# Attention on one Trainium2 core: products of probabilities and values for two key tiles in one burst

## The reference, cut to what matters

```
x = x + attention0(layernorm(x), ctx, mask)        # stage xa0: cross attention, masked
x = x + block(layernorm(x))                        # stage sa0: self attention, then 8 experts (me0)
x = x + attention1(layernorm(x), ctx)              # stage xa1: cross attention
x = x + experts(x)                                 # me1

def attention(Q, K, V, mask, W_Q, W_K, W_V, W_O):
    q, k, v = split_heads(Q @ W_Q.T), split_heads(K @ W_K.T), split_heads(V @ W_V.T)
    scores = einsum('bhqd,bhkd->bhqk', q, k) / sqrt(DK)
    weights = softmax(where(mask == 0, -inf, scores))
    return merge_heads(einsum('bhqk,bhkd->bhqd', weights, v)) @ W_O.T
```

## Time and profile before

| what | value |
| --- | --- |
| median of 3 runs | 1273.53 us (1271.52 to 1274.54) |
| the profiled execution, its own time | 1274.43 us |
| its span | 1272.7 us |
| TensorE matmul busy | 1131.4 us, 89% of the span |
| VectorE busy | 838.6 us, 66% |
| ScalarE busy | 660.4 us, 52% |
| L985, 1536 records | 204.9 us busy, mean 605 ns |
| L958, 720 records, and L971, 768 | 280.9 and 294.3 us busy |

### The profile page before, as it was taken

The page is one execution under the profiler, slowest core; times in us unless marked ns, Lnnn a source line. Parts: engine busy times, 40 slices in busy tenths (PEclk is TensorE's granted clock), DMA queues, the critical chain, the costliest instruction groups (busy, mean ns, idle before and its releaser), DMA issues. The chain is left out here.

```text
span 1272.7 us, 17810 instructions
## 1 busy us (share of the span) xinstructions
PE 1131.4 (89%) x5693; PEld 544.0 (43%) x5722; DVE 838.6 (66%) x2112; ACT 660.4 (52%) x1341; POOL 210.9 (17%) x272
## 2 busy tenths in 40 slices
PE   7889999999997999999967999996989999998390
PEld 4423343434453223343364666664523333335370
DVE  5878777777478888888762222223888888876722
ACT  3346666666533677677722333332537767674250
POOL 4310000000143000000202222211520010102154
PEclk9989999999999899999967999998989999999795
DMA  8953321221048433543291140103873323211064
GB/s 265 309 169 93 79 57 28 81 52 26 2 154 291 103 91 90 132 97 93 72 375 33 31 161 28 27 13 102 263 241 91 90 59 89 60 37 57 25 171 144
DMA packets 100706, 139.40 MB, mean 110 GB/s; under 512 B 8452, under 2 KB 82632, under 8 KB 99208
## 3 DMA queue, kind: packets, MB, share of 16 engines
q1 hardware_dynamic: 96536, 128.03, 33.6%
q0 software_dynamic: 4080, 10.23, 2.9%
HBM read 86.30 MB, written 52.17 MB: 109 GB/s over the span
## 5 line engine op out<-in xcount | busy, mean ns | idle before, releaser
L885 ACT ACTIVATE r<-ps 128x512 f32<-128x512 f32 x768 | 427.4, 600 | 211.9 <-PE ps L971 122.1
L377 DVE TENSOR_REDUCE m<-ps 128x1 f32<-128x512 f32 x512 | 320.9, 682 | 45.2 <-PE ps L958 44.9
L971 PE MATMUL ps<-r 99*128 99x512 bf16 x768 | 294.3, 388 | 5.6 <-ACT r L885 5.6
L958 PE MATMUL ps<-r 96*128 96x512 bf16 x720 | 280.9, 393 | 20.5 <-DVE m L377 7.0
L373 DVE CUSTOM_DVE_ANT_0 r<-ps,r 128x512 bf16<-128x512 f32 x256 | 170.2, 690 | 60.2 <-PE ps L958 59.6
L985 PE MATMUL ps<-r 128*32 128x512 f32 x1536 | 204.9, 605 | 4.9 <-ACT r L885 3.3
L971 PEld LDWEIGHTS ps<-r 99*128 99x128 bf16 x768 | 74.4, 98 | 211.7 <-ACT r L885 157.3
L958 PEld LDWEIGHTS ps<-r 96*128 96x128 bf16 x720 | 71.3, 99 | 105.9 <-DVE m L377 24.3
L861 POOL COPY r<-r 128x256 f32<-128x256 f32 x48 | 19.0, 399 | 542.1 <-PE ps L985 542.1
L1660 DVE COPY r<-ps 128x512 f32<-128x512 f32 x46 | 31.8, 691 | 91.9 <-PE ps L1707 91.9
L1707 PE MATMUL ps<-r 128*128 x184 | 87.8, 621 | 2.7 <-issue 0.4
(11 more groups left out here) (151 smaller groups left out, 1220.5 us busy)
## 6 DMA issues: line engine op xcount, KB each, us to landing
r<-q_parts SPq DMA_DIRECT2D x48, 384.0 KB, 5.2
r<-k_parts SPq DMA_DIRECT2D x48, 384.0 KB, 6.0
k_parts<-r SPq DMA_DIRECT2D x24, 384.0 KB, 3.3
q_parts<-r SPq DMA_DIRECT2D x24, 384.0 KB, 3.1
r<-in_w SPq DMA_DIRECT2D x16, 512.0 KB, 4.9
r<-in_w SPq DMA_DIRECT2D x8, 1024.0 KB, 14.4
k_parts<-r SPq DMA_DIRECT2D x24, 256.0 KB, 3.3
q_parts<-r SPq DMA_DIRECT2D x24, 256.0 KB, 3.1
```

Source lines behind the costliest of these rows:

```text
L377: ins = dve.tensor_reduce(out, mem.ps[:, bank, :], AX.X, ALU.max)
L885: act.activation(mem.probs[:, u // HG, u % HG, :], ps[:, ST + (UNITS * g + u) % DEEP, :], ACT.Exp, scale=SCALE).then_inc(a.p_exp.sem, 1)
L958: pe.matmul(ps[:, led_bank(n), :], mem.qst[g][0:ROWS, h, t * P:(t + 1) * P], mem.kst[g][0:ROWS, h, :], start=True, stop=True).then_inc(a.s ...
L971: ins = pe.matmul(out, mem.kst[g][0:KROWS, h, kt * P:(kt + 1) * P], mem.qst[g][0:KROWS, h, :], start=True, stop=not a.masked)
```

## The change

`products` now makes two key tiles (`TOGETHER` = 2), eight matmuls in a row. It stands behind unit 9 for key tiles 0 and 1, and behind unit 1 of the next group for key tiles 2 and 3; the calls behind units 5 and 13 are gone. It waits for the exponentials of both key tiles before its first matmul. The semaphore `pv` still counts each key tile. At the end of a stage the last call makes two key tiles as well.

```
--- before.py
+++ after.py
@@ -754,6 +754,7 @@
 HALF_TURN = (3, 13)
 LAST_TURN, LAST_OUT = (5, 2), (3, 4)
 LATE = 2
+TOGETHER = 2
 
 M_STEP, TURN_STEP = 8, 12
 OUT_TURNS = (3, 5)
@@ -976,15 +977,16 @@
                             start=False, stop=True)
         ins.then_inc(a.st_ps.sem, 1)
 
-    def products(G, g, kt):
-        pe.wait_ge(a.p_exp.sem, a.p_exp.at(G, HG * (kt + 1)))
-        if kt == 0:
+    def products(G, g, first):
+        pe.wait_ge(a.p_exp.sem, a.p_exp.at(G, HG * (first + TOGETHER)))
+        if first == 0:
             pe.wait_ge(a.vg_ready.sem, a.vg_ready.at(G, 1))
             pe.wait_ge(a.ot_sb.sem, a.ot_sb.at(G))
-        for h in range(HG):
-            ins = pe.matmul(ps[h * VW:(h + 1) * VW, OB, :], mem.vg[g % 2][:, kt, h, :], mem.probs[:, kt, h, :],
-                            start=(kt == 0), stop=(kt == T - 1))
-        ins.then_inc(a.pv.sem, 1)
+        for kt in range(first, first + TOGETHER):
+            for h in range(HG):
+                ins = pe.matmul(ps[h * VW:(h + 1) * VW, OB, :], mem.vg[g % 2][:, kt, h, :], mem.probs[:, kt, h, :],
+                                start=(kt == 0), stop=(kt == T - 1))
+            ins.then_inc(a.pv.sem, 1)
 
     def maxima(G):
         pe.wait_ge(a.cut.sem, a.cut.at(G, CUTS))
@@ -1056,11 +1058,11 @@
                     used = before(b, UNITS * g + u)
                     scores(s, v, UNITS * g + u, (used[0], used[1] + LEAD))
 
-                at = u - HG - LATE + 1
-                if at < 0 and u == LATE - 1 and not (first and g == 0):
-                    products(G - 1, (g - 1) % NG, T - 1)
-                if at >= 0 and at % HG == 0:
-                    products(G, g, at // HG)
+                at = u + 1 - LATE
+                if at == 0 and not (first and g == 0):
+                    products(G - 1, (g - 1) % NG, T - TOGETHER)
+                if at > 0 and at % (TOGETHER * HG) == 0:
+                    products(G, g, at // HG - TOGETHER)
                 if g == 1 and not first and u in OUT_TURNS:
                     turn_out(b - 1, OUT_TURNS.index(u))
                 if u == M_STEP and not (last and g == NG - 1):
@@ -1100,7 +1102,7 @@
         body(b, False, False)
     body(B - 1, False, True)
     G = B * NG - 1
-    products(G, NG - 1, T - 1)
+    products(G, NG - 1, T - TOGETHER)
     turn(G)
     meanwhile()
     for c in range(1, C):
```

## The result

The changed kernel takes 1310.3 us (median of 4, 1304.99 to 1313.14) against 1274.03 for the kernel before on the same chip: a ratio of 1.028, interval 1.025 to 1.032, so 36 us slower. Forecast were 1306, 32 us slower.

A forecast was written before the change was run, and what follows sets the result against it. TensorE bounds the kernel, but merged bursts starve it through VectorE's slower maxima: 32.6 us in the unmasked stages, −2 in the first, +1.5 at stage ends, sum 32, so 1306 us; range 1288 to 1320.

The forecast's parts named there:

- What binds whom: Unmasked stages: TensorE sets the time; its bursts let VectorE (0.60 us per maximum against 0.44 per unit) catch up.
- The double burst: Two key tiles in one burst: lasts 1.90 us, saving 0.19 us per pair of bursts.
- Run B: Unmasked units 10 to 15, 0 and 1: eighth L958 waits for VectorE; 6.88 us instead of 6.12, 0.76 slower.
- Plain group: Unmasked group without other work, runs of 7.09 and 6.88 us: grows from 12.2 to 14.0 us.
- the walk: Step-by-step timing of eight-unit unmasked runs from trace spacings: units 2 to 9 lose 1.00 us, units 10 to 1 0.76.
- Over a batch boundary: First unit of a batch reuses the bank of the unit just before: 0.15 us more, three times per unmasked stage, 0.5.
- Groups with output tiles: Groups 2 and 3, units 2 to 9: 0.90 us slower in the second stage, 0 in the last.
- First stage: Masked stage: 28 double bursts save 5.3 us, against 2.4 for banks between batches and about 1 for mask copies; net −2.
- rival 2: Unmasked stages: waits of about 1 us per run drop TensorE's clock to 1.2 GHz in places; 1335 us; chance 0.04.
- Rival 1: All stages: TensorE stays the bound, every double burst among scores saves 0.19 us, nothing waits; 1258 us; chance 0.08.
- Rival 3: Inside a double burst the second quad doesn't follow directly: 2.18 us instead of 1.90, 24 more; 1330 us; chance 0.04.
- Rival 4: Waits and savings cancel: waits a quarter of those forecast, time within 0.2%, 1271 to 1276 us; chance 0.04.

The follow-up runs named there:

- e3: The changed kernel with maxima over half of the columns in the two unmasked stages; 1259.63 us, ratio 0.989 to the kernel before.
- e5: The changed kernel with double bursts behind units 13 and 5 and stacks loaded one group earlier; 1270.78 us, ratio 0.998 to the kernel before.
- e1: The kernel before with double bursts in the masked first stage alone, other two attention stages unchanged; 1265.17 us, ratio 0.992.

## Why the prediction was right, point by point

- **What binds whom: right.** TensorE set the time before, and only because single bursts let VectorE catch up. e3 (shorter maxima) and e5 (other places) both take the loss away with the double bursts in place. TensorE's busy share in the last stage fell to 91% and VectorE's to 79%, as forecast.
- **The double burst: right, a little long.** 1.86 instead of 1.90. The drain at a change of tiling that the Trainium skill describes ("TensorEngine Tiling (Array Packing)", Key Properties) would be saved once per pair. The trace agrees as far as it goes: groups of the masked stage with the output's turns went from 16.66 to 16.14, 0.26 per pair where I had 0.19; it shows the spacing of the records, not a drain by itself.
- **Run B: right.** 6.79 against 6.88. **Plain group: right in itself**, 13.85 against 7.09 + 6.88 = 13.97, but the kernel before had 12.69 and 12.84 there and not the walk's 12.21, so the loss is 1.0 to 1.2 and not 1.76. It waited for stacks, as I had seen, but I took only 0.2 per group off for that. Over a batch boundary the last stage lost 1.53 where my terms give 1.91; that remainder I haven't traced. Groups with the output's turns lost 0.84 (forecast 0.88).
- **Groups with output tiles.** Last stage 0.65 more (forecast 0.76), second stage 1.52 more (forecast 0.90 + 0.76 = 1.66).
- **First stage: sign right, size wrong.** Forecast −2, measured −6.4, and −7.5 in e1. The two terms against the saving hold: the copies of the mask cost 0.9 in the third group (15.74 before, 16.15 after, two L959 behind L373 late by 0.46 and 0.41; I had about 1), and a group over a batch boundary lost 0.15 where my terms, the bank less the saving, give 0.4. Too small was the saving, 0.24 to 0.26 per pair instead of 0.19, 7 us instead of 5.3. Left out were a wait of 0.8 for stacks (L958 at 97.53) that the changed kernel hasn't, and the burst that leaves the way to group 0: this way is 1.5 shorter, of which the burst is 1.31 − 0.22 = 1.1 by my estimate. It comes back behind the last L995, where it costs nothing: from there to the next stage's first L995 it is 90.61 before, 90.47 in the change and 90.66 in e1. For the ends I had added 0.5 per stage.
- **The clock: a term left out.** I priced it in rival 2 and gave it 0.04; it came in part, 9.6 us beside the forecast mechanism. By my own sign, a clock below 1.00 in these stretches, the forecast didn't hold in parts of the second stage (0.76 and 0.78). The Trainium skill's case of small waits between groups of matmuls ("TensorE: Matmul & The Clock Gate", A second HAM failure mode: psum-queue depth-cycling) fits what is seen here, five falls in the second stage and one in the last; 1060 to 1115 us stays at 1.00 although the eighth L959 of a run comes 0.9 late.
- **So the 32 is partly right by offset, that is by luck.** In the profiled execution, second and last stage without the clock's 9.6: 15.4 and 13.5, together 28.9, forecast 32.6. First stage −6.4 for −2. Clock +9.6 for 0. The rest +6.6 for 1.5, of which 3.5 before any changed instruction. Sum 38.7 of span.
- **Rival 1** (TensorE stays the bound) fell where there is no mask and is what happens in the masked stage. **Rival 3** (second quad doesn't follow) fell with 1.86. **Rival 4** (waits and savings cancel) fell with the ratio of 1.028.

## What to carry to other kernels

Work of one engine that looks like a plain cost can be the slack in which another engine, or a DMA, catches up. Before merging or moving it, walk one stretch between bursts with the buffers' depth: the pace of producer and consumer, and where the consumer's extra work falls. Here merging is right where the producer is slower than the consumer (TensorE's 0.66 us per unit against 0.61 from one masked maximum to the next, 253.92 to 254.53 in the kernel before; 7.5 us less for that stage in e1) and wrong where it is faster (0.44 against 0.60).

## What was not expected of the hardware

- The clock of TensorE fell to half for stretches of 3.4 us in the middle of stages: twice behind a wait of 1.66 us, which stands in two more places without a fall, and four times behind waits of 0.57 and 1.0 us at a batch boundary, out of six. From 1060 to 1115 us, with an L959 some 0.9 late in most runs (the eighth at 1097.53) and one such boundary (L959 at 1083.25), it stayed at 1.00. What exactly makes it fall stays open.
- Passes of quads in the same column tiles follow each other at 0.43 us (first records at 1091.52, 1091.95 and 1092.37 in the last stage) after 0.45 between the first two (1091.06 to 1091.52); that is why a double burst is shorter than three times 0.45 and 0.55.
